# Dealing out the P times V matmuls of an attention ring singly, and moving the full fp32 units and the pairs with a difference into the same slots

## What is computed

```python
h = _layernorm(x, ln1_g, ln1_b)
q = (h @ Wq).reshape(Bb, Ss, H, Dh)
k = (h @ Wk).reshape(Bb, Ss, H, Dh)
v = (h @ Wv).reshape(Bb, Ss, H, Dh)
scores = jnp.einsum('bqhd,bkhd->bhqk', q, k) / jnp.sqrt(jnp.float32(Dh))
attn = jax.nn.softmax(scores, axis=-1)
ctx = jnp.einsum('bhqk,bkhd->bqhd', attn, v).reshape(Bb, Ss, Dd)
x = x + ctx @ Wo
```

## Time and profile before

| | before |
|---|---|
| median of 3 runs | 4740.93 us (4733.44 to 4748.56) |
| the profiled execution's own time | 4736.03 us |
| its span | 4734.2 us |
| TensorE busy | 4110.2 us (87%) |
| GpSimd busy | 3356.3 us (71%) |
| VectorE busy | 2870.3 us (61%) |
| ScalarE busy | 2803.7 us (59%) |

### The profile page before, as it was taken

The page is one execution under the profiler, slowest core; times in us unless marked ns, Lnnn a source line. Parts: engine busy times, 40 slices in busy tenths (PEclk is TensorE's granted clock), DMA queues, the critical chain, the costliest instruction groups (busy, mean ns, idle before and its releaser), DMA issues. The chain is left out here.

```text
span 4734.2 us, 80747 instructions
## 1 busy us (share of the span) xinstructions
PE 4110.2 (87%) x21172; PEld 1951.4 (41%) x21172; DVE 2870.3 (61%) x5778; ACT 2803.7 (59%) x3421; POOL 3356.3 (71%) x1877
## 2 busy tenths in 40 slices
PE   7569999999999999999999999999999983499991
PEld 4333333333333333333333333333333343499991
DVE  3447666667666666766766777667666644133335
ACT  1226766667666666666666777667666641255550
POOL 0017787777778777877777787778787764788875
PEclk8778999999999999999998999999999995799995
DMA  2331101010101010110101010101010024344433
GB/s 79 124 104 20 19 9 21 9 19 10 19 9 20 9 19 9 21 19 9 21 9 19 9 20 9 20 10 19 10 20 9 9 77 157 123 139 139 139 116 116
DMA packets 145755, 205.72 MB, mean 43 GB/s; under 512 B 43537, under 2 KB 108433, under 8 KB 140177
## 3 DMA queue, kind: packets, MB, share of 16 engines
q1 hardware_dynamic: 127072, 173.76, 13.5%
q0 software_dynamic: 6336, 16.79, 1.1%
q10 hardware_dynamic: 12144, 12.06, 0.7%
HBM read 134.59 MB, written 66.85 MB: 43 GB/s over the span
## 5 line engine op out<-in xcount | busy, mean ns | idle before, releaser
L623 POOL TENSOR_TENSOR probs_low<-probs 128x1024 f16<-128x1024 f32 x1408 | 2636.7, 1893 | 803.2 <-ACT probs L761 799.6
L761 ACT ACTIVATE probs<-s_ps 128x1024 f32<-128x1024 f32 x2048 | 2070.6, 1024 | 656.6 <-PE s_ps L673 652.6
L795 DVE TENSOR_REDUCE unit_max<-m_ps 128x1 f32<-128x512 f32 x2816 | 1799.6, 684 | 510.1 <-PE m_ps L665 483.5
L665 PE MATMUL m_ps<-k_ring,q_stage 48*128 48x512 f32 x3456 | 1134.3, 440 | 261.7 <-DVE unit_max L789 152.3
L673 PE MATMUL s_ps<-q_stage,k_ring 50*128 50x512 f32 x4096 | 1037.1, 488 | 15.5 <-issue 15.2
L673 PEld LDWEIGHTS s_ps<-q_stage,k_ring 50*128 50x128 f32 x4096 | 400.3, 189 | 1020.6 <-ACT probs L761 541.2
L665 PEld LDWEIGHTS m_ps<-k_ring,q_stage 48*128 48x128 f32 x3456 | 535.7, 195 | 623.0 <-DVE unit_max L789 318.1
L789 DVE CUSTOM_DVE_ANT_0 excess<-m_ps,excess 128x512 f32<-128x512 f32 x640 | 442.6, 692 | 571.6 <-ACT excess L748 559.0
L690 PE MATMUL o_ps<-probs,v_full 128*64 128x512 f32 x2560 | 735.7, 654 | 0.0
L748 ACT ACTIVATE excess<-m_ps 128x512 f32<-128x512 f32 x640 | 380.8, 595 | 449.9 <-PE m_ps L665 449.6
L696 PE MATMUL o_ps<-probs,v_parts 128*64 128x512 bf16 x2816 | 594.9, 419 | 0.5 <-ACT probs L761 0.3
(11 more groups left out here) (194 smaller groups left out, 3588.9 us busy)
## 6 DMA issues: line engine op xcount, KB each, us to landing
w_in<-in_W SPq DMA_DIRECT2D x46, 1024.0 KB, 4.9
q_stage<-max_turned SPq DMA_DIRECT2D x2048, 0.5 KB
q_stage<-qs_dram SPq DMA_DIRECT2D x768, 32.0 KB, 1.8
k_ring<-ks_dram SPq DMA_DIRECT2D x96, 128.0 KB, 4.3
slots_dram<-zero_rows SPq DMA_DIRECT2D x24, 512.0 KB, 6.5
rows_e<-slots_dram SPq DMA_DIRECT2D x24, 512.0 KB, 3.9
y_slots_dram<-y_out ACTq DMA_DIRECT2D x23, 512.0 KB, 4.2
qs_dram<-parts SPq DMA_DIRECT2D x16, 512.0 KB, 2.8
```

The lines of the kernel that those rows point to most:

```text
L623: nc.gpsimd.tensor_tensor(probs_low[:, POOL_UNITS.index(t), :, :], probs[:, t, :, :], high_view[:, t, :, :, 1], ALU.subtract).then_inc(poo ...
L665: nc.tensor.matmul(m_ps[:, b % 3, :], q_stage[at:at + SROWS, col:col + P], ring[at:at + SROWS, par, key:key + CHUNK], start=True, stop=Tru ...
L761: nc.scalar.activation(probs[:, t, :, :], s_ps[:, t % 2, :, :], ACT.Exp).then_inc(exp_done, 1)
L795: nc.vector.tensor_reduce(unit_max[:, b, qt, 2 * j + k:2 * j + k + 1], m_ps[:, block_of(t, k) % 3, :], AX.X, ALU.max).then_inc(m_read, 1 + ...
```

## The change

The computation stays as it is; only places in the order change.

- The five full fp32 units and the eleven split ones stay the same units. Before there are 11 visits, five of them with two split units, in slots 10, 12, 14, 15, 0, 2, 3, 4, 6, 7 and 8. Now there are 14 visits: the full units 3, 6, 9, 12 and 15 in slots 12, 15, 2, 5 and 8, one split unit each in slots 13, 14, 0, 1, 3, 4 and 6, and two in slots 10 and 7. Of the 16 slots, 9 has no visit and 11 has the turn.
- The pairs with a difference move from slots 1, 4, 7, 10 and 14 to slots 2, 5, 8, 12 and 15. These are the slots of the full units.
- The rest of the diff is a frame for making low parts on VectorE, which is switched off (`DVE_UNITS` is empty), and the flag that closes the accumulation on the last unit, now a full one.

```diff
-POOL_UNITS = tuple(t for t in range(UNITS) if t not in FULL_UNITS)
-VISITS = ((0, 1), (3,), (2, 4), (6,), (5, 7), (9,), (8, 10), (12,), (11, 13), (15,), (14,))
-SLOTS = (10, 12, 14, 15, 16, 18, 19, 20, 22, 23, 24)
+DVE_UNITS = ()
+LOW_UNITS = tuple(t for t in range(UNITS) if t not in FULL_UNITS)
+POOL_UNITS = tuple(t for t in LOW_UNITS if t not in DVE_UNITS)
+DVE_PLACES = {}
+VISITS = ((0, 1), (3,), (2,), (4,), (6,), (5,), (7,), (9,), (8,), (10,), (12,), (11,), (13, 14), (15,))
+SLOTS = (10, 12, 13, 14, 15, 16, 17, 18, 19, 20, 21, 22, 23, 24)
 COPY_SLOT, TURN_SLOT = 8, 11
-RELU_PAIRS = (1, 4, 7, 10, 14)
+RELU_PAIRS = (2, 5, 8, 12, 15)
...
                     if t in FULL_UNITS:
                         for k in range(2):
                             last = nc.tensor.matmul(o_ps[V_COLS * k:V_COLS * k + V_COLS, :],
                                                     v_full[:, par, FULL_UNITS.index(t), k, :], probs[:, t, k, :],
-                                                    start=False, stop=False)
+                                                    start=False, stop=final)
```

More of the change, by code:

```diff
@@ L484, in softmax_attention @@
         probs = sb("probs", [P, UNITS, 2, CHUNK])
-        probs_low = sb("probs_low", [P, len(POOL_UNITS), 2, CHUNK], F16)
+        probs_low = sb("probs_low", [P, len(LOW_UNITS), 2, CHUNK], F16)
         no_max = sb("no_max", [P, TPC])
@@ L503, in softmax_attention @@
         s_done, exp_done, pv_done = sem("s_done"), sem("exp_done"), sem("pv_done")
-        pool_low_done = sem("pool_low_done")
+        pool_low_done, dve_low_done = sem("pool_low_done"), sem("dve_low_done")
         m_done, m_read, excess_ready = sem("m_done"), sem("m_read"), sem("excess_ready")
@@ L622, in split_probs @@
                     pool.wait_ge(exp_done, i * UNITS + (t + 1))
-                    nc.gpsimd.tensor_tensor(probs_low[:, POOL_UNITS.index(t), :, :], probs[:, t, :, :],
+                    nc.gpsimd.tensor_tensor(probs_low[:, LOW_UNITS.index(t), :, :], probs[:, t, :, :],
                                             high_view[:, t, :, :, 1], ALU.subtract).then_inc(pool_low_done, 1)
@@ L686, in values @@
                         pe.wait_ge(pool_low_done, i * len(POOL_UNITS) + (POOL_UNITS.index(t) + 1))
+                    if t in DVE_UNITS:
+                        pe.wait_ge(dve_low_done, i * (2 * len(DVE_UNITS)) + 2 * (DVE_UNITS.index(t) + 1))
                     first, final = t == VISITS[0][0], t == VISITS[-1][-1]
@@ L691, in values @@
                                                     v_full[:, par, FULL_UNITS.index(t), k, :], probs[:, t, k, :],
-                                                    start=False, stop=False)
+                                                    start=False, stop=final)
                         continue
-                    for n, part in enumerate((high_view[:, t, :, :, 1], probs_low[:, POOL_UNITS.index(t), :, :])):
+                    for n, part in enumerate((high_view[:, t, :, :, 1], probs_low[:, LOW_UNITS.index(t), :, :])):
                         for k in range(2):
@@ L823, in finish_max, with low, chunk @@
                                         max_parts[:, :, :].bitcast(F32).rearrange("p r n -> p (r n)")).then_inc(max_ready, 1)
-            def chunk(n, b, ahead=True, finish=True, turn=True, stores=None):
+            def low(i, t, k):
+                dve.wait_ge(exp_done, i * UNITS + (t + 1))
+                nc.vector.tensor_tensor(probs_low[:, LOW_UNITS.index(t), k, :], probs[:, t, k, :], high_view[:, t, k, :, 1],
+                                        ALU.subtract).then_inc(dve_low_done, 1)
+            def chunk(n, b, ahead=True, finish=True, turn=True, stores=None, current=True):
                 for t in range(UNITS):
@@ L837, in chunk @@
                             dve.sem_inc(m_read, RING_BLOCKS - 1 - TURN_BLOCK)
+                    if current and t in DVE_PLACES:
+                        low(n - LEAD, *DVE_PLACES[t])
                     if finish and not ahead and t == FINISH_SLOTS[0]:
@@ L841, in chunk @@
                         finish_max(n - 1, 1 - b, FINISH_SLOTS.index(t))
-            chunk(0, 0, finish=False, turn=False)
-            chunk(1, 1, turn=False)
+            chunk(0, 0, finish=False, turn=False, current=False)
+            chunk(1, 1, turn=False, current=False)
             chunk(2, 0, turn=False)
@@ L853, in _ @@
             chunk(RING + 1, 1, ahead=False, finish=False, stores=RING // 2 - 1)
-            chunk(RING + 2, 0, ahead=False, finish=False, stores=RING // 2 - 1)
+            chunk(RING + 2, 0, ahead=False, finish=False, stores=RING // 2 - 1, current=False)
 def row_statistics(nc, dve, ch, stats, mean_var, std, rstd, var_ready, std_ready, n):
```

## The result

The changed kernel takes 4793.75 us in the median (4 runs, 4778.63 to 4809.8) against 4744.75 us for the kernel before beside it (4 runs, 4733.44 to 4752.22): a ratio of 1.0106, 95% interval 1.0065 to 1.0146. It is slower by about 1.1%. 4726 with a range of 4655 to 4790 was forecast, so the forecast had the wrong sign, and the time lies 4 us above its range.

The account below looks back on a forecast made before the run. No engine is full; TensorE is paced by its own queue and, at places, by the reading of `m_ps`. 124 x 26.5 + 64 + 34 = 3384 against 3399, 15 less: 4721, median 4726, range 4655 to 4790.

Parts of the forecast that it names:

- The slots: Slot times of a chunk at full clock, summed without the holds: 25.28 us, 1.02 less than 26.30.
- the new wait: VectorE's steps 1 and 2 held until GpSimd's low parts end: 1.44 us a chunk, 25.28 to 26.72.
- Holds without falls: Rival: VectorE's steps are held, but the clock never falls outside the returns; 3320, total 4662; chance 0.10.
- the ring: The 124 chunks between first and last steady turn: 3399 us before, 3384 forecast after.
- VectorE gets in first: Rival: VectorE's step 1 reaches the ports before GpSimd's unit 1; 3169, 230 less, total 4511; chance 0.10.
- the 0.11 us that I had: In slot 1, VectorE's step 1 comes at 3.69, 0.11 us too late against GpSimd's unit 1 at 3.58.
- I take the falls to go on: Clock falls around TensorE's waits in slots 3 and 4: 41 of 108 delayed chunks, 1.56 us each, 64 us.
- The slower rival: Rival: the clock falls in all 108 delayed chunks; 3488, 89 more, total 4830; chance 0.10.

Follow-up runs that it names:

- doubles behind full units: Changed kernel with eleven visits again, split units in pairs in the slot behind a full unit, single only in slot 7: 4919.01 us, ratio 1.0357.
- the extra scores in slot 5: Changed kernel with the scores of unit 5 computed three times over, same result: 4799.05 us, ratio 1.0108.

## Why the prediction was wrong

**What held.** The slots: 25.28 us summed, 24.97 to 25.1 measured in the three free chunks and 25.2 in the kernel with steps 0 and 1 in front. The mechanism of the new wait, by its steps: L818 at 1.87 us (1.8 foretold), L822 at 1.32 (1.3), the wait in slot 3 at 0.84 (0.8), ended by L794, none of 1.20 there, undisturbed chunks of 26.72 (26.72), GpSimd's low parts at 1.89. Holds without falls: 3322.8 in the ring (3320). The rival "VectorE gets in first": 3169 was given, and the kernels in which it does stand at 3157 to 3161, and at 3194.5 where step 2 is still held behind the split of V. It does get in first in three of the changed kernel's chunks. The margin was smaller than the 0.11 us that I had: 0.03, mostly since slot 1 starts 1.65 us behind slot 0 and not 1.71 (517.49 to 519.14).

By the Trainium skill's page SBUF — State Buffer, section Who interferes with whom, the shared ports go for the whole instruction to whichever engine issues first. The trace agrees for VectorE: started 0.03 us late, step 1 takes 1.72 us more; started 0.02 us early, it takes its 0.15. That GpSimd is held in the second case no row here shows: its low part takes 1.90 us there (the row at 416.80) and 1.89 elsewhere.

**What failed.** The step "I take the falls to go on: estimated for 41 of the 108 delayed chunks, 1.56 us each, 64 us". The number was near, and that was luck, since nothing in its working gave it: 47 falls outside the loop's returns. The price was not. I took it from the falls of before, where the clock comes back after 3.4 us. After, it is away for 6.8 or 10.2 us and a fall costs 2.45 or 4.0 us. The ring with falls less the ring without is 129 us, twice the 64, or 2.7 us a fall. Of the 68 us by which the ring missed its sum (3452 against 3384), 65 are this term.

**The slower rival.** "Slower: in all 108 delayed chunks the clock falls", deciding from 51 falls at 1.56. It got the sign from its mechanism, falls of the clock behind the holds, but not from its number: 47 chunks had a fall, not 108, and at 1.56 us each they would have given 3320 + 73 = 3393, about the ring of before. One of its sums is off too: the range's end at 4790 answers to 82 falls at that price ((4790 - 4662) / 1.56), not to about 90.

**Where the gain went.** Nothing held, the change is worth 3398.9 - 3161.3 = 238 us of the ring. 162 of them go to the holds (3322.8 - 3161.3) and 129 to the falls that they start: 53 us slower. Moving VectorE's steps 0 and 1 in front of slot 0's pair gives all of it back.

**What stays open.** Why a fall lasts 3.4, 6.8 or 10.2 us. That the falls of the changed kernel need the wait of slot 3 is shown: six extra matmuls there end them with the holds in place, four in slot 5 don't. That such a wait is enough isn't: about 100 chunks have it and 47 have a fall, and with the pairs alone moved waits of 1.2 us start few. That the work behind it bears on its length is shown in part by the extra scores in slot 5. Which property of this work counts was not found: single units against doubles went against what I thought. Nor is it shown why long falls come in several neighbouring chunks at a time, at the same place in each.

## What to carry to other kernels

Where an instruction of 0.16 us can be held for 1.9 by another engine, its place in the queue counts and not its duration: look at what starts within some tenths of a microsecond of it, and put it where the other engine is idle. A clock fall's price holds only for the place where it was read: when the work around it moves, bound it from both sides like a price never seen. When a change loses, run each of its parts alone and with the new wait removed: here the part that lost 96 us with the hold was worth 163 without.

## What the runs showed of the hardware that I had not expected

- A `tensor_scalar` of 4 elements with one input in SBUF was held for 1.87 us, as the form with two inputs was (1.87). A reduction of 32 elements in SBUF, started inside a GpSimd instruction, took 0.18 us.
- The granted clock stayed at 0.50 through 6.8 us and more in which TensorE's records fill all the time, and 56 times in one ring, that with doubles behind full units, for 10.2 us.
- 744 additional matmuls, in a wait of TensorE, made the kernel 120 us faster.
- The six returns of the PE loop with their falls don't cost the same in each kernel. Over six undisturbed chunks they take 35 us more before the change and 24 after it, 45 and 47 in the two kernels with the new visits and the old pairs (chunks of up to 37.2 us), 26 to 32 in the four kernels with a chunk of 25.2, and 10 with the pairs alone. Why is open.
